# A mixture-of-experts layer behind a time-mixing layer: expert choice behind the scores, slot assignment behind the value mixes, GpSimd's scatters spread

## The chip, the cores and the metric

The kernel runs on one core of one Trainium2 chip. The metric is the device time in microseconds (us) of one execution, as the median of several. The engines of the core are named as in the profile: PE (TensorE, matmuls; PEld is its weight load), DVE (VectorE), ACT (ScalarE), POOL (GpSimd) and SP (SyncE, which issues most DMAs). Each has its own instruction stream and waits for others by semaphores.

## The reference, cut to what matters

```python
x = L0_attn_x                                # 8 x 512 x 512, float32
xn = _layernorm(x)
x = x + attn(xn) + ffn(xn)

# attn: prev = xn shifted by one step, xx = prev - xn
r, k, v, g = (xn + xx*tm_i) @ W_i.T          # four mixes, four 512 x 512 projections
# a scan over time of exp(k) and exp(k)*v, times sigmoid(r) and sigmoid(g), then @ Wo.T, layer norm

# ffn: z = w_norm * rmsnorm(xn), 4096 tokens
probs = softmax(z @ w_router)                # 32 experts
w_topk, sel = top_k(probs, 4)
pos = rank of a (token, choice) among those of its expert, in token order   # kept if pos < 256
y = (silu(buf @ w_gate) * (buf @ w_up)) @ w_down      # for each expert, on its up to 256 rows
out = sum of y over a token's experts by weight + sigmoid(z @ w_shared_gate) * shared_ffn(z)
```

## The kernel before, in words

The program has three stages, one after the other, each with a barrier of all engines at its end. The change lies in the first, `project_stage`; the second, `expert_stage`, begins by reading back from device memory the table of which token sits in which slot of which expert, gathers the rows of the first two experts by it, and transposes them. The third makes the shared part and the output.

The first stage runs over the 8 batches b of 512 tokens (round b); the first and last are written out, the rest are a loop of two rounds a turn. `one_round` of each engine's block is an instruction order written out by hand, so the order in the code is the order on the engine, and an instruction that waits holds all behind it on its engine.

All matmuls that need float32 precision are made as three matmuls of a high and a low part. For each of the four mixes i = K_, V_, R_, G_ and each of four chunks k: DVE makes `mixf` (`make_mix`), ACT rounds it to the high part (`mix_hi`), POOL subtracts to get the low part (`mix_lo`), and PE multiplies (`project`, in two halves, "pairs", of 24 matmuls each; pair 0 needs the low part of each chunk k in turn). What waits for what around the change:

- PE's order in round b: K pair 0, K pair 1, V pair 0, the two matmuls of `count(b)`, transposes `tz` and `ta` of token tile 0 of batch b+1, V pair 1, transposes of tile 1, R pair 0, `score(b+1, 0)`, transposes of tile 2, R pair 1, `score(b+1, 1)`, transposes of tile 3, G pair 0, `score(b+1, 2)` and `(b+1, 3)`, G pair 1. So the scores of a batch are complete one G pair before its own round.
- The four accumulators pj[m] are shared by all projections. K pair 0 of round b may write pj[0] and pj[1] only when DVE has read them in `make_gate(b-1, 0)` and `(b-1, 1)`.
- `choose(b)` on DVE (L540 to L564) turns scores into the four experts of each token and the running counts. `count(b)` on PE turns those into ranks. `assign(b)` on DVE (L576 to L598) makes slot numbers and weights. `scatter` on POOL then writes token numbers into their slots by 16 indirect DMAs a round.
- `norm_stats(b+1)` on DVE (L486, L489) feeds `norm_scales(b+1)` on POOL (L296 to L305), which stands ahead of the low parts of V of round b, since ACT needs the scales for `make_xn(b+1, ...)` and DVE then for `make_z(b+1, ...)` (L497), whose tile PE transposes.
- `route_exp(b)` on ACT takes the exponentials for the weights and needs what `choose(b)` leaves in `sh`.

The wait of PE for the accumulators is this:

```python
            def taken(b, i, m):
                if i == K_:
                    wait(pe, gate_made, b * 4 - 3 + m if not isinstance(b, int) or b else 0)
                else:
                    pe.wait_ge((None, ek_made, ekv_made, sr_made)[i], b * 4 + m + 1)
```

Of the kernel before, what the change touches and what calls it, by code (L numbers as in the profile page):

```python
# [28 lines left out]
KC = C // P  # L29
# [12 lines left out]
K_, V_, R_, G_ = range(4)  # L42
# [46 lines left out]
def project_stage(nc, keep, d):  # L89

    with ExitStack() as ctx:
# [192 lines left out]
        @block.gpsimd  # L284
        def _(pool):
            pows = Steps(pool, pow_step, POWS)

            def norm_scales(b):

                wait(pool, scales_kept, b)  # L290
                wait(pool, z_made, b * NT)
                wait_apart(pool, (setup_pool, 4), stats_step, (b + 1) * STATS)
                mean, var = mv[:, :, 0], mv[:, :, 1]
                rstd, shift = scales[:, 0:NT], scales[:, NT:2 * NT]
                pows.round(b)
                pows.link(pool.tensor_scalar(var_eps[:], var, EPS, None, ALU.add))  # L296
                pows.link(pool.tensor_tensor(rstd, var_eps[:], mhalf[:], ALU.pow))
                pows.step(pool.tensor_tensor(shift, mean, rstd, ALU.mult))
                pows.step(pool.tensor_tensor(var_eps[:], rstd, rstd, ALU.mult))
                pows.join_apart((setup_pool, 4))  # L300
                pows.step(pool.tensor_scalar(shift, shift, -1.0, None, ALU.mult))
                pows.step(pool.tensor_tensor(var_eps[:], var_eps[:], var, ALU.mult))
                pows.join_apart((setup_pool, 4))
                pows.link(pool.tensor_scalar(var_eps[:], var_eps[:], EPS_RMS, None, ALU.add))
                pows.step(pool.tensor_tensor(r2[:], var_eps[:], mhalf[:], ALU.pow))  # L305
                pows.end()

            def mix_lo(b, i, k):
                n = b * 16 + i * 4 + k
                pool.wait_ge(hi_made, n + 1)  # L310
                pool.tensor_tensor(mix[:, i % 2, k, 1, :], mixf[:, k, :], mix[:, i % 2, k, 0, :].bitcast(F32),  # L311
                                   ALU.subtract).then_inc(lo_made, 1)

            def scatter(b, first, last):

                if first == 0:
                    wait_apart(pool, (setup_pool, 4), slot_made, b + 1)
                for at in range(first, last):
                    pool.indirect_dma_start(  # L319
                        d["slots"], bass.IndirectOffsetOnAxis(ap=slot[:, at:at + 1], axis=0),  # L320
                        token[:, at // TOPK:at // TOPK + 1], None, bounds_check=SLOTS - 1, oob_is_err=False,
                    ).then_inc(scattered, 16)

            pool.memset(zero_tab[:], 0).then_inc(setup_pool, 1)
            pool.memset(mhalf[:], -0.5).then_inc(setup_pool, 1)
            pool.memset(ones[:], 1.0).then_inc(setup_pool, 1)
            pool.memset(seen[:], 0.0).then_inc(setup_pool, 1)
            pool.wait_ge(setup_pool, 4)
            norm_scales(0)
            for k in range(KC):  # L330
                mix_lo(0, K_, k)
            pool.wait_ge(table_zeroed, 16)

            def one_round(b, half, more, before):
                if more:
                    norm_scales(b + 1)
                for k in range(KC):
                    mix_lo(b, V_, k)
                for k in range(KC):
                    mix_lo(b, R_, k)  # L340
                scatter(b, 0, 4)
                for k in range(KC):
                    mix_lo(b, G_, k)
                scatter(b, 4, 12)
                if more:
                    for k in range(KC):
                        mix_lo(b + 1, K_, k)
                scatter(b, 12, 16)

            rounds(pool, one_round)  # L350
            pool.wait_ge(scattered, 16 * B * NT * TOPK)

        @block.scalar
        def _(act):
# [74 lines left out]
            def one_round(b, half, more, before):  # L429
                if before:  # L430
                    gate_g(b - 1, 2)
                    gate_g(b - 1, 3)
                for k in range(KC):
                    mix_hi(b, V_, k)
                exp_k(b, 0)
                exp_k(b, 1)
                if not before:
                    weight_hi(R_)
                if more:
                    make_xn(b + 1, 0)  # L440
                    make_xn(b + 1, 1)
                exp_k(b, 2)
                exp_k(b, 3)
                route_exp(b)
                for k in range(KC):
                    mix_hi(b, R_, k)
                if not before:
                    weight_hi(G_)
                if more:
                    keep_turned(b + 1, 1 - half, 0)  # L450
                    make_xn(b + 1, 2)
                    keep_turned(b + 1, 1 - half, 1)
                    make_xn(b + 1, 3)
                for k in range(KC):
                    mix_hi(b, G_, k)
                gate_r(b, 0)
                gate_r(b, 1)
                if more:
                    keep_turned(b + 1, 1 - half, 2)
                gate_r(b, 2)  # L460
                gate_r(b, 3)
                if more:
                    keep_turned(b + 1, 1 - half, 3)
                    mix_hi(b + 1, K_, 0)
                    mix_hi(b + 1, K_, 1)
                gate_g(b, 0)
                gate_g(b, 1)
                if more:
                    mix_hi(b + 1, K_, 2)
                    mix_hi(b + 1, K_, 3)  # L470
# [6 lines left out]
        def _(dve):  # L477
# [146 lines left out]
            for k in range(KC):  # L624
                make_mix(0, 0, K_, k)
            weight_lo(V_)

            def one_round(b, half, more, before):
                if more:
# [3 lines left out]
                    make_gate(b - 1, 3)  # L633
                for k in range(KC):
                    make_mix(b, half, V_, k)
                choose(b)
                if not before:
                    weight_lo(R_)
                make_mix(b, half, R_, 0)
# [9 lines left out]
                    z_lo(b + 1, 0)  # L649
                if not before:  # L650
                    weight_lo(G_)
                assign(b)
                make_ekv(b, 2)
                make_ekv(b, 3)
                if more:
# [9 lines left out]
                if more:  # L665
                    z_lo(b + 1, 2)
                    z_lo(b + 1, 3)
                    for k in range(KC):
                        shift_difference(b + 1, 1 - half, k)
                    make_mix(b + 1, 1 - half, K_, 0)  # L670
                    make_mix(b + 1, 1 - half, K_, 1)
                make_gate(b, 0)
                make_gate(b, 1)
                if more:
# [8 lines left out]
        def _(pe):  # L683
# [66 lines left out]

            def one_round(b, half, more, before):
                project(b, K_, 0)
                project(b, K_, 1)
                project(b, V_, 0)
                count(b)
                if more:
                    turn_z(b + 1, 0)
                    turn_xn(b + 1, 0)
# [992 lines left out]
```

## Time and profile before

| | us |
|---|---|
| median of 3 runs (1802.17 to 1803.08) | 1802.35 |
| the profiled execution, its own time | 1808.25 |
| its span, first to last instruction | 1806.4 |
| PE busy in the span | 1697.6 (94%) |
| DVE busy | 1239.6 (69%) |
| POOL busy | 872.0 (48%) |
| ACT busy | 662.2 (37%) |
| first stage, about | 0 to 488 |

Busy time is the sum over the whole span, and PE is nearly always busy. So what counts in the first stage is where PE stands still, and for whom. The granted clock, a mean over the span, is 0.973 of full speed.

### The profile page before, as it was taken

The numbers are of one execution on the slowest core, as the hardware profiler recorded it, in microseconds if no ns is written. First come the engines' busy times: TensorE is split into PE (matmuls) and PEld (weight loads), VectorE is DVE, ScalarE is ACT, GpSimd is POOL, SyncE is SP. The second block draws the span as 40 slices with busy tenths as digits, with TensorE's granted clock in tenths as the row PEclk, the third lists the DMA queues.
The fourth block names the chain that finished last, engine by engine and source line by source line (L and its number), as shares of the span: only waits on it lengthen the run. The fifth ranks groups of instructions, "written<-read, shape, count | busy, mean of one in ns | idle before, by whom it ended". The sixth has DMA issues, their size and how long they took to land. (4 is left out here: it accounts for less than half of the span.)

```text
span 1806.4 us, 26943 instructions
## 1 busy us (share of the span) xinstructions
PE 1697.6 (94%) x8752; PEld 1445.4 (80%) x8752; DVE 1239.6 (69%) x1798; ACT 662.2 (37%) x1083; POOL 872.0 (48%) x727
## 2 busy tenths in 40 slices
PE   4899999999589999999986889999999999999998
PEld 4687787778489999999974768888788888888887
DVE  4887787877255555555545778877686868777776
ACT  3444444454256656666642321212121211212121
POOL 2678777777644454454423524334252524334251
PEclk7999999999889999999997999999999999999999
DMA  6233333333276666666637665455554443343431
GB/s 221 94 136 129 134 139 141 139 116 116 103 257 225 231 251 229 226 250 235 221 112 265 192 204 179 150 198 174 165 164 139 151 147 110 110 161 117 141 108 50
DMA packets 130475, 299.43 MB, mean 166 GB/s; under 512 B 23692, under 2 KB 35212, under 8 KB 129872
## 3 DMA queue, kind: packets, MB, share of 16 engines
q1 hardware_dynamic: 110928, 264.64, 41.6%
q0 software_dynamic: 19456, 33.67, 6.6%
q8 instruction: 45, 0.74, 0.2%
q14 instruction: 46, 0.38, 0.1%
HBM read 233.64 MB, written 81.36 MB: 174 GB/s over the span
## 5 line engine op out<-in xcount | busy, mean ns | idle before, releaser
L738 PE MATMUL pj<-mix,w 128*128 128x512 f32 x1536 | 377.7, 403 | 14.1 <-POOL mix L311 12.2
L738 PEld LDWEIGHTS pj<-mix,w 128*128 128x128 f32 x1536 | 290.0, 191 | 87.1 <-issue 10.7
L1616 PE MATMUL s_gp<-s_zT,s_wg 128*128 128x512 f32 x1056 | 265.1, 402 | 38.4 <-DVE s_wg L1524 22.3
L1616 PEld LDWEIGHTS s_gp<-s_zT,s_wg 128*128 128x128 f32 x1056 | 204.6, 195 | 85.1 <-DVE s_wg L1524 25.1
L1630 PE MATMUL s_yp<-s_wd,s_h 128*128 128x512 f32 x1056 | 254.1, 390 | 0.6 <-DVE s_h L1433 0.6
L1616 PE MATMUL s_up<-s_zT,s_wu 128*128 128x512 f32 x1056 | 253.9, 389 | 0.0
L1630 PEld LDWEIGHTS s_yp<-s_wd,s_h 128*128 128x128 f32 x1056 | 198.1, 188 | 42.6 <-issue 1.2
L1616 PEld LDWEIGHTS s_up<-s_zT,s_wu 128*128 128x128 f32 x1056 | 198.7, 188 | 41.5
L876 POOL TENSOR_TENSOR e_wg<-e_g_in,e_wg 128x1408 fp32r<-128x1408 f32 x32 | 103.5, 3233 | 214.4 <-ACT e_wg L896 214.4
L311 POOL TENSOR_TENSOR mix<-mixf,mix 128x512 fp32r<-128x512 f32 x128 | 174.1, 1389 | 67.4 <-ACT mix L385 67.2
L1275 POOL DMA_INDIRECT s_picked<-y_rows,s_slot x128 | 144.3, 1128 | 83.8 <-DVE s_total L1483 45.6
L319 POOL DMA_INDIRECT slot_tokens<-token,slot x128 | 134.0, 1047 | 63.6 <-issue 36.5
L1348 ACT ACTIVATE s_act_g<-s_gp 128x512 f32<-128x512 f32 x88 | 52.5, 597 | 301.5 <-PE s_gp L1616 294.9
L1034 PE MATMUL e_gu<-e_xT,e_wg 128*128 128x256 f32 (+1 forms) x1152 | 153.4, 283 | 2.4 <-DVE e_xT L980 2.4
L1034 PE MATMUL e_gu<-e_xT,e_wu 128*128 128x256 f32 (+1 forms) x1152 | 152.5, 282 | 0.0
L1359 ACT ACTIVATE s_h<-s_act_g 128x512 fp32r<-128x512 f32 x88 | 55.5, 631 | 259.5 <-DVE s_act_g L1427 250.9
L1034 PEld LDWEIGHTS e_gu<-e_xT,e_wg 128*128 128x128 f32 (+1 forms) x1152 | 145.4, 181 | 5.4 <-DVE e_xT L980 2.8
L385 ACT ACTIVATE mix<-mixf 128x512 fp32r<-128x512 f32 x128 | 80.8, 633 | 185.0 <-DVE mixf L521 151.9
L1034 PEld LDWEIGHTS e_gu<-e_xT,e_wu 128*128 128x128 f32 (+1 forms) x1152 | 142.6, 180 | 0.0
L1057 PE MATMUL e_yp<-e_wd,e_h 128*128 128x512 f32 (+1 forms) x576 | 140.1, 396 | 0.0
L1483 DVE SCALAR_TENSOR_TENSOR s_total<-s_picked,s_rec,s_total 128x512 f32<-128x512 f32 x128 | 135.4, 1058 | 3.4
L1057 PEld LDWEIGHTS e_yp<-e_wd,e_h 128*128 128x128 f32 (+1 forms) x576 | 106.3, 189 | 21.4
(148 smaller groups left out, 2392.1 us busy)
## 6 DMA issues: line engine op xcount, KB each, us to landing
s_wu<-wu_split SPq DMA_DIRECT2D x77, 512.0 KB
e_g_in<-in_w_gate SPq DMA_DIRECT2D x32, 704.0 KB
e_u_in<-in_w_up SPq DMA_DIRECT2D x32, 704.0 KB
zT_tiles<-zT SPq DMA_DIRECT2D x32, 512.0 KB
e_d_in<-in_w_down SPq DMA_DIRECT2D x32, 512.0 KB
y_rows<-e_y SPq DMA_DIRECT2D x32, 512.0 KB, 2.9
s_zT<-zT_tiles SPq DMA_DIRECT2D x32, 512.0 KB, 5.8
x_in<-in_x SPq DMA_DIRECT2D x32, 256.0 KB
```

The costliest lines, as they stand in the source:

```text
L311: pool.tensor_tensor(mix[:, i % 2, k, 1, :], mixf[:, k, :], mix[:, i % 2, k, 0, :].bitcast(F32), ALU.subtract).then_inc(lo_made, 1)
L319: pool.indirect_dma_start(d["slots"], bass.IndirectOffsetOnAxis(ap=slot[:, at:at + 1], axis=0), token[:, at // TOPK:at // TOPK + 1], None, ...
L385: act.activation(mix[:, i % 2, k, 0, :], mixf[:, k, :], ACT.Copy).then_inc(hi_made, 1)
L738: last = pe.matmul(pj[m][:], w[i][:, w_part, k, m * P:(m + 1) * P], mix[:, i % 2, k, x_part, :], start=(k == 0 and q == 0), stop=(k == KC ...
L876: pool.tensor_tensor(wg[:, half, 1, :], g_in[:, half, :], wg[:, half, 0, :].bitcast(F32), ALU.subtract).then_inc(wg_lo, 1)
L1034: last = pe.matmul(gu[f][0:m, which, :], w[:, half, w_part, k * F + f0:k * F + f0 + m], xT[:, half, x_part, k, :], start=(q == 0 and k == ...
L1057: last = pe.matmul(yp[c][:], h[0:m, f, h_part, c * P:(c + 1) * P], wd[0:m, half, w_part, f, :], start=(f == 0 and q == 0), stop=(f == NF - ...
L1275: pool.indirect_dma_start(picked[:, k, :], None, d["y_flat"], bass.IndirectOffsetOnAxis(ap=slot[:, j * TOPK + k:j * TOPK + k + 1], axis=0) ...
L1359: act.activation(h[:, i, 0, :], act_g[:, i, :], ACT.Copy).then_inc(h_hi, 1)
L1483: dve.scalar_tensor_tensor(total[:, j, :], picked[:, k, :], rec[:, at:at + 1], total[:, j, :], ALU.mult, ALU.add).then_inc(picked_used, 1)
L1616: last = pe.matmul(bank[:], parts[w_part][:, k, :], zT[:, :, x_part, k, :], start=(q == 0 and k == 0), stop=(q == 2 and k == KC - 1))
L1630: last = pe.matmul(yp[j][:], h[:, i, h_part, j * P:(j + 1) * P], wd[:, w_part, f, :], start=(f == 0 and q == 0), stop=(f == NFS - 1 and q ...
```

## The change

It reorders instructions and adds or removes none. On DVE `choose(b+1)` moves from behind the V mixes of its own round into the round before, right behind the first two K mixes of b+1 and ahead of `make_gate(b, 0)` and the other two K mixes; for the first batch it stands ahead of the first round. `assign(b)` takes the place that `choose(b)` had. `count(b)` on PE moves from behind V pair 0 to between the two K pairs. On ACT `route_exp(b)` moves ahead of the exponentials of the second K pair. On POOL the scatters, which stood in blocks of 4, 8 and 4 (behind the R low parts, the G low parts and the K low parts of b+1), now stand as 3, 2, 4, 2 and 5, between pairs of low parts, all ahead of the K low parts of b+1.

```diff
 # POOL, one_round
                 for k in range(KC):
                     mix_lo(b, V_, k)
-                for k in range(KC):
-                    mix_lo(b, R_, k)
-                scatter(b, 0, 4)
-                for k in range(KC):
-                    mix_lo(b, G_, k)
-                scatter(b, 4, 12)
+                scatter(b, 0, 3)
+                mix_lo(b, R_, 0)
+                mix_lo(b, R_, 1)
+                scatter(b, 3, 5)
+                mix_lo(b, R_, 2)
+                mix_lo(b, R_, 3)
+                scatter(b, 5, 9)
+                mix_lo(b, G_, 0)
+                mix_lo(b, G_, 1)
+                scatter(b, 9, 11)
+                mix_lo(b, G_, 2)
+                mix_lo(b, G_, 3)
+                scatter(b, 11, 16)
                 if more:
                     for k in range(KC):
                         mix_lo(b + 1, K_, k)
-                scatter(b, 12, 16)
 # ACT, one_round
                 exp_k(b, 1)
+                route_exp(b)
...
                 exp_k(b, 3)
-                route_exp(b)
 # DVE, ahead of the rounds and in one_round
             weight_lo(V_)
+            choose(0)
...
                 for k in range(KC):
                     make_mix(b, half, V_, k)
-                choose(b)
+                assign(b)
...
                 if not before:
                     weight_lo(G_)
-                assign(b)
                 make_ekv(b, 2)
...
                     make_mix(b + 1, 1 - half, K_, 0)
                     make_mix(b + 1, 1 - half, K_, 1)
+                    choose(b + 1)
                 make_gate(b, 0)
                 make_gate(b, 1)
 # PE, one_round
                 project(b, K_, 0)
+                count(b)
                 project(b, K_, 1)
                 project(b, V_, 0)
-                count(b)
```

DVE's order at the end of the first round (`xx` is the shifted difference, `mixf` a mix, `sr` the gate product, `lg` to `seen` the choice). Before:

```order
L507 TENSOR_TENSOR zT<-tz,zT 128x512 x2
L513 TENSOR_TENSOR xx<-xnT 128x512 x4
L521 SCALAR_TENSOR_TENSOR mixf<-xx,tm,xnT 128x512 x2
L533 TENSOR_TENSOR sr<-sr,pj 128x512 x2
L521 SCALAR_TENSOR_TENSOR mixf<-xx,tm,xnT 128x512 x2
```

And now, with lines of the changed file:

```order
L527 SCALAR_TENSOR_TENSOR mixf<-xx,tm,xnT 128x512 x2
L546 COPY lg<-rp 128x136
L548 TENSOR_TENSOR lg<-lg,rp 128x136
L551 MAX v<-lg 128x8 x4
L554 MAX_INDEX i<-v,lg 128x8 x4
...
L562 TENSOR_TENSOR oh<-idxf,const 128x512
L566 TENSOR_REDUCE chosen<-oh 128x128
...
L570 TENSOR_TENSOR seen<-seen,chosen 128x32 x4
L539 TENSOR_TENSOR sr<-sr,pj 128x512 x2
L527 SCALAR_TENSOR_TENSOR mixf<-xx,tm,xnT 128x512 x2
```

The whole choice now stands ahead of the two gate products and of the last two K mixes.

DVE's order behind the V mixes of the first round. Before, the choice and then, after the low part of a weight (`w`), the R mixes and the tiles `z`:

```order
L521 SCALAR_TENSOR_TENSOR mixf<-xx,tm,xnT 128x512 x4
L540 COPY lg<-rp 128x136
...
L564 TENSOR_TENSOR seen<-seen,chosen 128x32 x4
L612 TENSOR_TENSOR w<-sr,w 128x2048
L521 SCALAR_TENSOR_TENSOR mixf<-xx,tm,xnT 128x512 x2
L497 SCALAR_TENSOR_TENSOR z<-xn,r,norm_w 128x512 x2
```

And now:

```order
L527 SCALAR_TENSOR_TENSOR mixf<-xx,tm,xnT 128x512 x4
L582 TENSOR_TENSOR oh<-oh,rp 128x512
L584 TENSOR_REDUCE pos<-oh 128x16
L585 TENSOR_SCALAR valid<-pos 128x16
...
L604 COPY keep_rec<-rec 128x20
L618 TENSOR_TENSOR w<-sr,w 128x2048
L527 SCALAR_TENSOR_TENSOR mixf<-xx,tm,xnT 128x512 x2
L503 SCALAR_TENSOR_TENSOR z<-xn,r,norm_w 128x512 x2
```

The assignment, two instructions on 512 elements and 15 on a few, stands where the choice stood; what follows is the same.

POOL's order in the first round, from its last scale (`r`) on (`mix` a low part, `slot_tokens` a scatter). Before:

```order
L305 TENSOR_TENSOR r<-var_eps,mhalf 128x4
L311 TENSOR_TENSOR mix<-mixf,mix 128x512 x8
L319 DMA slot_tokens<-token,slot 8192x1 x4
L311 TENSOR_TENSOR mix<-mixf,mix 128x512 x4
L319 DMA slot_tokens<-token,slot 8192x1 x8
L311 TENSOR_TENSOR mix<-mixf,mix 128x512 x4
L319 DMA slot_tokens<-token,slot 8192x1 x4
```

And now:

```order
L311 TENSOR_TENSOR mix<-mixf,mix 128x512 x4
L319 DMA slot_tokens<-token,slot 8192x1 x3
L311 TENSOR_TENSOR mix<-mixf,mix 128x512 x2
L319 DMA slot_tokens<-token,slot 8192x1 x2
L311 TENSOR_TENSOR mix<-mixf,mix 128x512 x2
L319 DMA slot_tokens<-token,slot 8192x1 x4
L311 TENSOR_TENSOR mix<-mixf,mix 128x512 x2
L319 DMA slot_tokens<-token,slot 8192x1 x2
L311 TENSOR_TENSOR mix<-mixf,mix 128x512 x2
L319 DMA slot_tokens<-token,slot 8192x1 x5
L311 TENSOR_TENSOR mix<-mixf,mix 128x512 x4
```

No scatter stands between the K low parts of the next batch and its scales any more; 3 stand ahead of the R low parts, and 5 of the 16, not 12, behind the last G low part.

## Rows read from the trace of the kernel before

**Rows 1.** Who PE waited for, 40 to 480 us: total, times, longest

```profile
PE pj L738 <- POOL mix L311: 8.5, 5, 2.0
```

**Rows 2.** PE's timeline: start, us, engine, line, what, count, idle before

```profile
121.60 0.23 PE L717 MATMUL rp<-chosen,before 128*128 128x128 bf16 x1
...
225.75 5.86 PE L738 MATMUL pj<-mix,w 128*128 128x512 f32 x24 [1.98 <-POOL mix L311]
...
260.19 1.87 PE L708 MATMUL rp<-wr,zT 128*128 128x68 f32 x16
261.90 17.04 PE L738 MATMUL pj<-mix,w 128*128 128x512 f32 x72
280.74 7.41 PE L738 MATMUL pj<-mix,w 128*128 128x512 f32 x24 [1.80 <-POOL mix L311]
...
397.57 0.23 PE L717 MATMUL rp<-chosen,before 128*128 128x128 bf16 x1
...
450.04 0.23 PE L717 MATMUL rp<-chosen,before 128*128 128x128 bf16 x1
```

**Rows 3.** A stretch behind a wait: us, PE busy (x), PEclk, DMA share, GB/s

```profile
282.00:285.40 3.40, 3.40 (x9) 0.50 0.00 0
```

**Rows 4.** POOL's timeline behind the K low parts, round 3

```profile
214.60 0.99 POOL L319 DMA_INDIRECT slot_tokens<-token,slot  x1 [0.15 <-issue]
...
219.65 0.50 POOL L296 TENSOR_SCALAR var_eps<-mv 128x4 f32<-128x4 f32 x1
...
224.36 5.02 POOL L311 TENSOR_TENSOR mix<-mixf,mix 128x512 fp32r<-128x512 f32 x4
```

**Rows 5.** DVE's timeline: the choice (round 1), and around it and assignment (round 3)

```profile
108.62 0.29 DVE L540 COPY lg<-rp 128x136 f32<-128x136 f32 x1
...
113.16 0.81 DVE L564 TENSOR_TENSOR seen<-seen,chosen 128x32 bf16<-128x32 bf16 x4
...
224.45 4.96 DVE L564 TENSOR_TENSOR seen<-seen,chosen 128x32 bf16<-128x32 bf16 x4
229.33 1.40 DVE L521 SCALAR_TENSOR_TENSOR mixf<-xx,tm,xnT 128x512 f32<-128x512 f32 x2
230.66 2.43 DVE L497 SCALAR_TENSOR_TENSOR z<-xn,r,norm_w 128x512 f32<-128x512 f32 x2
...
237.79 0.68 DVE L576 TENSOR_TENSOR oh<-oh,rp 128x512 f32<-128x512 f32 x1
...
241.49 0.18 DVE L598 COPY keep_rec<-rec 128x20 f32 x1
...
262.05 1.28 DVE L533 TENSOR_TENSOR sr<-sr,pj 128x512 f32<-128x512 f32 x2 [1.25 <-issue]
```

**Rows 6.** ACT's high parts, 40 to 480 us, by line: busy, mean ns, idle

```profile
L385 ACT ACTIVATE mix<-mixf 128x512 fp32r<-128x512 f32 x124 | 78.3, 633 | 180.0 <-DVE mixf L521 147.0 <-issue 30.6
```

**Rows 7.** One line of DVE: duration ns least/median/most, first and last start

```profile
L578 DVE TENSOR_REDUCE pos<-oh x8: 685/686/686, 73.1 to 454.0; 128x16 f32<-128x512 f32 x8
```

**Rows 8.** Timelines of DVE and PE in the first round

```profile
43.47 2.46 DVE L486 BATCH_NORM_STATS2 st<-x_in 128x6 f32<-128x512 f32 x4
...
52.84 5.96 PE L738 MATMUL pj<-mix,w 128*128 128x512 f32 x24 [1.44 <-issue]
...
57.72 2.28 DVE L612 TENSOR_TENSOR w<-sr,w 128x2048 fp32r<-128x2048 f32 x1
...
62.04 0.75 PE L690 MATMUL tz<-const,z 128*128 128x128 f32 x4 [3.12 <-DVE z L497]
...
89.33 0.72 PE L690 MATMUL ta<-const,xn 128*128 128x128 f32 x4 [2.61 <-ACT xnT L372]
89.81 5.52 PE L738 MATMUL pj<-mix,w 128*128 128x512 f32 x16
```

**Rows 9.** The end of the stage: POOL's last scatter, and who SP waited for

```profile
484.40 0.97 POOL L319 DMA_INDIRECT slot_tokens<-token,slot  x1 [0.30 <-issue]
...
SPq L91 <- PEq L91: 3.8, 1, 3.8
```

## The prediction

> **What bounds the kernel now.** PE is busy for 94% of the span, so I read only its gaps. The list of who PE waited for gives the recurring one: five waits for POOL's low parts, 8.5 us together [rows 1]. PE's timeline puts them at the start of V pair 0 (225.75, 280.74) [rows 2]. What all gaps of the steady rounds cost follows from the repeating `count`: from 121.60 to 397.57 there are five intervals, 55.2 us each; the one to 450.04 takes 52.47, with the same matmuls and no wait ahead of V [rows 2]. So the five lose 5 x 2.73 = 13.6 us. About 8.5 are the waits; another 1.6 is the V pair behind one of them, 7.41 us where 225.75 shows 5.86 [rows 2]: PE's granted clock there is 0.50, the lower of its levels (1.2 GHz), right after it had stood still for 1.80 [rows 2, 3].
>
> Why PE waits is in POOL's timeline: four scatters from 214.60, the scales from 219.65, the first V low part from 224.36, 1.3 us long, when PE had been ready since 223.8 [rows 4]. In the last round the scales fall away, and so does the wait.
>
> **The change, part by part.** I count from E, the end of the last score of the next batch (262.06) [rows 2]. DVE's gate products started there at 262.05 [rows 5]. PE starts K pair 0 5.5 us behind E (a third of the 17.04 from 261.90) [rows 2].
>
> *The choice behind the scores.* It takes 108.62 to 113.97, 5.35 us, when POOL is not in low parts [rows 5]. Two K mixes, two gates and PE stand behind it. Gates: E+5.35 to E+6.65 (1.28 for two). K mixes 2 and 3, 0.7 each [rows 5]: E+7.35 and E+8.05. High part 0.63 [rows 6], low part 1.27 (5.02 for four) [rows 4], plus about 0.1 a hop: low part 2 at E+9.5, low part 3 at E+10.8. PE: first wait for the gate, start E+6.05, chunk 2 at E+9.5 where it would have been at 5.5+2.8 = E+8.3, chunk 3 at E+10.9, done E+12.35 for 11.2 without waits. **K pair 0 ends 1.1 us late in each of rounds 1 to 7: +7.7.** The choice meets only K low parts 0 and 1 on POOL, until about E+1.4. Its first instructions then read PSUM or one operand, and such ones were never held: the reduce L578 takes 685 to 686 ns in all rounds [rows 7]. The bound above is one held for those low parts, +0.75; below, a whole hidden half, if gates alone count, 0.5 in place of 1.1.
>
> *The V wait.* No scatters stand between the K low parts and the scales. Statistics follow K mix 3 (2.9 us as from 43.47 in the first round [rows 8]): E+11.0. Scales 4.7 (219.65 to 224.36) [rows 4]: E+15.7; V low part 0: E+17.0. PE, late as above, wants it at E+18.1. Covered, by 1.1 us. **All that the five intervals lose goes: -13.6.** If the cover is gone, part of the waits returns.
>
> *The assignment behind the V mixes.* Undisturbed it is 3.9 us, 237.79 to 241.67 [rows 5]. It starts at E+14.9, and POOL is in V low parts from E+15.7 to E+20.9. Short DVE instructions are held then: the four `seen` additions, 0.81 us alone, took 4.96 beside the low parts of 224.36 [rows 4, 5]. I therefore let only the first two and about four short instructions pass by E+20.9; 2.1 us are left. Behind them stand R mixes 0 and 1 (1.4) and the first `z` (0.75): ready at E+25.2. PE wants it when V pair 0 ends, E+18.1+5.7 = E+23.8. **A new wait of 1.3 to 1.4 us ahead of the transposes, in six rounds: +7.8.** Before, there was no such wait but no slack either: V pair 0 from 225.75 ended at 231.5, and `z` was there at 231.4 [rows 2, 5]; the difference is that the choice ended with the low parts, and the assignment has a tail beyond them. Bounds: 0 (the short ones slip through) to 2.1.
>
> The Trainium skill's page SBUF — State Buffer, section Who interferes with whom, has this as an exclusive port pair held for one whole instruction, against DVE's two-input and 2-port forms, with reduces free of it. The `seen` and reduce rows agree. Taken strictly, assignment loses a little less there than I charge, some 2 us over six rounds.
>
> *Scatters and what else moves.* 16 scatters a round of about 1.28 us each (start to start: four fill 214.60 to 219.65 [rows 4]) are the same work. Five of them behind the last G low part leave POOL free before the K high parts come, where eight did not; three ahead of the R low parts delay these by 3.8 us, some 4 us before PE wants them. `route_exp` finds its input long made. `count` between K pairs finds the choice made in rounds 1 to 7. All at nothing.
>
> *First round.* `choose(0)` now stands ahead of the statistics, which began at 43.47 [rows 8]. They end at 43.47+5.35+2.9 = 51.7, the scales at 56.4, V low part 0 at 57.7 for a V pair that started at 52.84 [rows 8]. PE stands still twice on the way (for the choice, ahead of `count(0)`, and for this). Then the low parts to 61.5, the rest of the assignment 1.0 (much of it passes before 56.4), the weight's low part 2.3 [rows 8], mixes 1.4, `z` 0.7: 66.9, where the transposes started at 62.04 [rows 8]: +4.9. The assignment is gone from the rest of the round, so the wait of 2.61 at 89.33 should go, and with it the slow 16 matmuls behind it, 5.52 where full clock gives 3.9 [rows 8]. **+4.9 - 2.6 - 1.6 = +0.7.** Bounds -2 to +5.
>
> *End of the stage.* POOL's last scatter begins at 484.40, and SP, done with its own, waits 3.8 us for the barrier [rows 9]. With 7 scatters fewer at the end (9 us) POOL is done before SP: **-3.8.**
>
> **Sum.** 7.7 + 7.8 - 13.6 + 0.7 - 3.8 = -1.2. The profiled execution took 1808.25 (span 1806.4), 5.9 above the median; all terms are differences in it, so I set them against the median: 1802.35 - 1.2 = **1801.2 us**. About 0.2%, 3.6 us, is what a measurement of this kernel tells from no change.
>
> **The rivals.**
>
> *The waits balance* (forecast, 0.42): 1797 to 1806. V waits of some 2.7 a round become 1.1 + 1.3.
>
> *The assignment slips through* (0.26): its short instructions run between low parts and no `z` wait arises. For it: DVE did get turns between low parts. Against: `seen`. Gives -1.2 - 7.8 = -9.0, 1793.3.
>
> *The clock falls more often* (0.18). PE now stands still twice a round, 13 times. Before, one of five waits of 1.4 to 2.0 us brought the lower clock, at 1.55 us [rows 2, 3]. Mine are shorter, and I charge none. If half of them bring it: 6 x 1.55 = +9.3, 1810.5.
> The page TensorE: Matmul & The Clock Gate of the same skill, section HAM oscillation — how this bites in real kernels, describes recurring waits that lower the clock each time; by that all 13 would, +20, which the trace so far doesn't bear out (one in five).
>
> *The choice is held on DVE* (0.14), the slower side in one mechanism: it stands ahead of what PE needs next, and K low parts 0 and 1 run as it begins. Held for 0.75 us it costs 7 x 0.75 = +5.2 (1806.5); held for both, 2.5 us, 7 x 2.5 = +17.5 (1818.7). It decides from 0.7 us a round on. For it: `seen`. Against: the kinds of instruction that come first.
>
> **Chances and range.** Faster by over 0.2% (below 1798.7): the slipping case and a tenth of the forecast's spread, 0.31. Within: 0.40. Slower (above 1806.0): the clock and the held choice, less their mild ends, 0.29. The range for 8 in 10 runs from the slipping case to the clock case, 1793 to 1810; the forecast's own is 1797 to 1806.
>
> **What would show it.** In the changed profile: no wait of PE for POOL ahead of V pair 0; ahead of K pair 0 one for DVE's gate and one for a K low part, together 1.1; one of 1.3 for `z` ahead of the transposes; `count` intervals of 54.9 us; SP's wait at the end gone. It is wrong if the interval comes out at 53.6 (no `z` wait) or above 56 (choice held, or the lower clock granted behind the new waits), or if the first round loses over 5 us.

## The result, and the profile after

The changed kernel takes **1808.49 us** (median of 18 runs, 1804.65 to 1811.28), the kernel before, run beside it, 1804.42 us (18 runs, 1802.17 to 1809.05). The ratio is 1.0022, 95% interval 1.0015 to 1.0029: slower by 0.22%, about 4 us, where no change to speak of was forecast (1801.2 us; 1808.5 lies within the range of 1793 to 1810).

The page's head and its row for PE:

```profile
span 1806.4 us, 26943 instructions
PE 1701.1 (94%) x8752; PEld 1445.0 (80%) x8752; DVE 1212.2 (67%) x1798; ACT 662.4 (37%) x1083; POOL 880.5 (49%) x727
```

The span is the same, to the tenth, as that of the profiled execution of before. Here that says nothing: the profiled execution of before (1808.25 us) lay far above its kernel's median, this one (1808.26 us) on its own. The stage that was changed has to be compared step by step, and with more than one execution of before.

Who PE waited for from 40 to 480 us, in total, times, longest, to be read against [rows 1] and [rows 8]; then who SP waited for at the end of the stage, against [rows 9]:

```profile
PE tz L697 <- DVE z L503: 4.9, 6, 2.0
PE pj L745 <- POOL mix L311: 4.8, 10, 1.5
PE pj L745 <- DVE sr L539: 4.7, 7, 2.4
PE rp L724 <- DVE seen L570: 4.2, 1, 4.2
...
SPq L91 <- PEq L91: 0.2, 1, 0.2
```

Of the 8.5 us of waits for POOL ahead of V pair 0, in five places, two waits of 0.3 are left; the rest of the 4.8 is six short waits within K pair 0 and two in the last round. Three new kinds stand there: DVE's gates seven times, `z` six times (2.04 in the first round, which waited for it before too, and five times later), the first choice once. SP hardly waits at the end. PE's timeline shows what a round looks like now (start, us, what, idle before and its releaser):

```profile
49.19 0.29 PE L724 MATMUL rp<-chosen,before 128*128 128x128 bf16 x1 [4.22 <-DVE seen L570]
...
66.14 0.75 PE L697 MATMUL tz<-const,z 128*128 128x128 f32 x4 [2.04 <-DVE z L503]
...
104.54 7.41 PE L745 MATMUL pj<-mix,w 128*128 128x512 f32 x24 [2.40 <-DVE sr L539]
111.78 0.23 PE L724 MATMUL rp<-chosen,before 128*128 128x128 bf16 x1
...
268.96 3.06 PE L745 MATMUL pj<-mix,w 128*128 128x512 f32 x12 [0.34 <-DVE sr L539]
272.26 3.06 PE L745 MATMUL pj<-mix,w 128*128 128x512 f32 x12 [0.24 <-POOL mix L311]
...
287.12 0.75 PE L697 MATMUL tz<-const,z 128*128 128x128 f32 x4 [0.42 <-DVE z L503]
...
384.68 0.23 PE L724 MATMUL rp<-chosen,before 128*128 128x128 bf16 x1
...
438.98 0.23 PE L724 MATMUL rp<-chosen,before 128*128 128x128 bf16 x1
...
460.39 11.46 PE L745 MATMUL pj<-mix,w 128*128 128x512 f32 x48 [1.49 <-POOL mix L311]
473.19 8.67 PE L745 MATMUL pj<-mix,w 128*128 128x512 f32 x36 [1.33 <-POOL mix L311]
```

A steady round (268.96, 272.26, 287.12) has the waits that were forecast: for the gate ahead of K pair 0, for a low part in its middle, for `z` ahead of the transposes. A wait costs more than its idle time. From the start of G pair 1 (262.77) to that of K pair 1 (275.26) it is 12.49 us; in the kernel before the same two pairs take 11.28, and `count` between them adds 0.10. That leaves 1.1 us for two waits with 0.58 us of idle time, so some 0.25 us come on top of each, which the rows show as busy. I call it draining; what it consists of the trace does not tell. Three places were not in the forecast: the gate's wait of 2.40 in round 1, with 24 matmuls of 7.41 us behind it (the others: 5.85), the lower clock behind the wait for the first choice, and two waits for POOL in the last round. The second of them, as a stretch (us, PE busy, PEclk; K pair 1 runs in it, and takes 8.14 us):

```profile
47.60:54.40 6.80, 5.21 (x14) 0.50 0.00 0
```

For the comparison I take, per kernel, the starts of `count` of each batch, and their distances:

| execution | from the second `count` on | first interval |
|---|---|---|
| before, [rows 2] | 54.66 55.20 56.53 54.16 55.42 52.47 | 62.96 |
| before, second (`before_again`) | 54.59 53.96 54.01 53.98 54.59 52.46 | 62.80 |
| before, third (`before_third`) | 54.60 53.96 54.53 53.93 54.61 52.46 | 62.94 |
| after | 53.57 54.32 55.49 54.30 55.22 54.30 | 62.59 |
| after, second (`after_again`) | 54.28 54.33 55.35 54.32 55.16 54.30 | 61.53 |

The distances of 56.53 and 55.42 that the prediction was made from are not there in the other two executions of before.

### The profile page after: what moved, and what is told of

It is laid out like the page before. It is cut to its first block and busy times, and to the rows that moved or that the text cites. A ratio compares the mean times of both kernels' runs of the same rounds, so it can differ in the third digit from the quotient of the medians.

```text
span 1806.4 us, 26943 instructions
## 1 busy us (share of the span) xinstructions
PE 1701.1 (94%) x8752; PEld 1445.0 (80%) x8752; DVE 1212.2 (67%) x1798; ACT 662.4 (37%) x1083; POOL 880.5 (49%) x727
## 5 line engine op out<-in xcount | busy, mean ns | idle before, releaser
L311 POOL TENSOR_TENSOR mix<-mixf,mix 128x512 fp32r<-128x512 f32 x128 | 164.5, 1317 | 70.0 <-ACT mix L391 69.6
L319 POOL DMA_INDIRECT slot_tokens<-token,slot x128 | 144.4, 1128 | 39.2 <-issue 37.8
```

The source lines that it names most:

```text
L319: pool.indirect_dma_start(d["slots"], bass.IndirectOffsetOnAxis(ap=slot[:, at:at + 1], axis=0), token[:, at // TOPK:at // TOPK + 1], None, ...
```

## The experiments

The question was where a gain of 13.6 us in the steady rounds had gone. The theories: the loss sits in the steady rounds (new waits at K and `z`), in round 1 (the choice held on DVE), or in the last round (scatters between the low parts). In kernels with `EARLY` and `SPREAD` the three flags are for the first, the middle and the last round, and switch the order of choice and assignment, and that of the scatters.

**The kernel before once more.** No edit.

> The kernel before, unchanged. The two profiled executions have the same span (1806.4 us) while the medians lie 4 us apart, so one of the profiles is not typical. Theory 1: the one of before is long by some 4 us, because of spells of the lower clock (three in its first stage); then this profile shows a span near 1802 to 1804, and the ratio of times is 1.000. Rival: the spans of profiles say nothing of the median and this one is 1806 again.

Measured: 1803.67 us, ratio 0.9998 (0.9988 to 1.0007). What PE waited for in its profile, 40 to 480 us:

```profile
PE pj L738 <- POOL mix L311: 5.4, 5, 1.4
PE tz L690 <- DVE z L497: 3.8, 2, 3.1
PE ta L690 <- ACT xnT L372: 2.6, 1, 2.6
```

Its profiled execution took 1802.74 us, with a span of 1800.9, so the first profile was the long one. The V waits come to 5.4 us, not 8.5, and PE's granted clock falls behind none of them, where it fell once in the first profile; the excess is thus mostly not the clock. The five steady intervals add up to 271.13 us, 8.8 more than 5 x 52.46. In the first profile DVE also stands for 1.46 and 1.65 us ahead of the statistics of rounds 3 and 5, with no releaser; in this one it does not. A third execution was taken for its intervals:

> The kernel before, a third profile. The forecast took from the first profile that five steady rounds lose 13.6 us; the second showed 8.8 (intervals of 54.0 to 54.6 us). Theory 1: the first was the odd one, this one shows 8 to 10 us again. Rival: the rounds really scatter between executions, and it lies anywhere from 8 to 14.

Its time was 1804.18 us, and its five lose 9.3. So there were about 9 us to be had from the steady rounds, not 13.6. Likewise the changed kernel again:

> The changed kernel, a second profile. Theory 1: the steady intervals repeat within 0.2 us (54.3, 55.5, 54.3, 55.3, 54.3), the last round has its two waits for R and G low parts (2.8 us) again, and the wait of 2.4 us for the gate in round 1, which hangs on how late POOL is there, lies between 1.2 and 2.5. Rival: any of these was of that one execution.

Its time was 1810.84 us. The waits stand in the same places, the gate's in round 1 too (2.39 us), this time with no slow matmuls behind it. The slow K pair 1 behind the first choice is there again (0.50 of the clock from 49 to 54).

**The choice behind the K mixes.** It tells what the choice costs where the change put it.

```diff
                     make_mix(b + 1, 1 - half, K_, 1)
-                    choose(b + 1)
                 make_gate(b, 0)
                 make_gate(b, 1)
                 if more:
                     make_mix(b + 1, 1 - half, K_, 2)
                     make_mix(b + 1, 1 - half, K_, 3)
+                    choose(b + 1)
```

> The changed kernel with the choice behind both gates and all four K mixes, still in the round before. Theory 1: the K waits (0.6 us a round, and 2.4 in round 1 with the lower clock behind it) go; but statistics and scales come some 4 us later against PE, so V low part 0 is late by some 2 us a round in rounds 1 to 6: in all 5 to 10 us slower than the changed kernel. Rival (the K waits are what counts): 6 us faster than it.

Measured: 1818.03 us, 1.0076 (1.0063 to 1.0090). The choice now delays the gates of the second half, which PE wants ahead of K pair 1:

```profile
PE pj L745 <- DVE sr L539: 12.8, 5, 3.9
```

The place that the change chose is the cheaper of the two. The kernel is 9.5 us above the changed one, within the 5 to 10 expected, but not for the reason expected: the V waits did not grow, PE waits 2.8 us for POOL in all. Two of the gate waits, 3.86 and 3.88 us, are 3 us longer than the two of 0.83 and 0.82 in the rounds behind them; in those two rounds DVE stands for 2.97 and 2.92 us with no releaser ahead of the statistics.

**The scatters as before.** The other half of the change undone.

```diff
-                scatter(b, 0, 3)
-                mix_lo(b, R_, 0)
...
-                scatter(b, 11, 16)
+                for k in range(KC):
+                    mix_lo(b, R_, k)
+                scatter(b, 0, 4)
+                for k in range(KC):
+                    mix_lo(b, G_, k)
+                scatter(b, 4, 12)
                 if more:
                     for k in range(KC):
                         mix_lo(b + 1, K_, k)
+                scatter(b, 12, 16)
```

> The changed kernel with the scatters of before (4, 8 and 4, the last four behind the K low parts). Theory 1: the last four scatters, 5.1 us, push the scales and V low part 0 from 17.0 to 22 us behind the end of the scores, where PE wants it at 18: a wait of 3 to 4 us ahead of V in rounds 1 to 6 and the clock falling behind some of them, so 15 to 25 us slower than the changed kernel. Rival (the scatters' places don't matter in the steady rounds): within 3 us of it.

Measured: 1832.87 us, 1.0154 (1.0138 to 1.0170). PE waits for POOL at V again, longer than before, and the lower clock comes back; the second fence is a stretch behind such a wait (us, PE busy, PEld, DVE, ACT, POOL, PEclk):

```profile
294.99 5.30 PE L739 MATMUL pj<-mix,w 128*128 128x512 f32 x15 [3.09 <-POOL mix L311]
```

```profile
295.00:299.00 4.00, 4.00 (x11) 3.15 (x12) 4.00 (x3) 2.61 (x5) 4.00 (x3) 0.57 0.00 0
```

The early choices with the old places of the scatters cost 28 us over before, within what was expected: four scatters still stand between the K low parts and the scales, and the statistics behind the choice come later than they did. The spread is what makes the move bearable.

**The scatters of the last round as before.**

```diff
+                if not more:
+                    for k in range(KC):
+                        mix_lo(b, R_, k)
+                    scatter(b, 0, 4)
+                    for k in range(KC):
+                        mix_lo(b, G_, k)
+                    scatter(b, 4, 16)
+                    return
                 scatter(b, 0, 3)
```

> The changed kernel, but in the last round all R low parts stand ahead of the first scatter and all G low parts behind the fourth, as before. Theory 1 (the last round's scatters between low parts cost PE 2.8 us of waits for R and G low parts, 3.2 us in all): faster than the changed kernel by 3 us, so level with before or up to 1 us above it; both waits gone; the gain at the stage's end stays. Rival (the 13 small waits of the steady rounds make the change slower): no more than 1 us faster than the changed kernel, 3 to 4 us slower than before.

Measured: 1805.93 us, 1.0011 (1.0002 to 1.0020). The changed kernel, measured in other runs, stands at 1.0022 (1.0015 to 1.0029) to the same kernel before; by these ratios it gains 2 us, and the two intervals overlap. PE runs through from 454.81 to its end, where the changed kernel stood still twice, 2.8 us together; SP waits 1.8 us again (3.3 to 3.8 before, 0.2 in the changed kernel), so not all of the gain at the end of the stage stays. In the traces the last round's R and G pairs are 3.3 us shorter and the end is 1.7 longer:

```profile
454.81 23.26 PE L753 MATMUL pj<-mix,w 128*128 128x512 f32 x99
```

```profile
SPq L91 <- PEq L91: 1.8, 1, 1.8
```

What POOL does there in the changed kernel:

```profile
445.99 0.99 POOL L319 DMA_INDIRECT slot_tokens<-token,slot  x1 [1.45 <-DVE slot L592]
451.77 0.98 POOL L319 DMA_INDIRECT slot_tokens<-token,slot  x1 [4.79 <-issue]
...
459.06 2.52 POOL L311 TENSOR_TENSOR mix<-mixf,mix 128x512 fp32r<-128x512 f32 x2
...
471.85 2.53 POOL L311 TENSOR_TENSOR mix<-mixf,mix 128x512 fp32r<-128x512 f32 x2
```

Behind the first scatter POOL stands for 4.79 us with no releaser, and the R low parts queue behind it: the last two end at 461.6, while PE had been ready for the first of them at 458.9. The G low parts are late in the same way. In the kernel before the R low parts stand ahead of the scatters, and the stop, 2.93 us there, holds up nothing that PE waits for.

**One stage of the change at a time.** The first round alone, the steady rounds alone, the last alone (its three last rounds written out instead of looped, with the scatters of before), and first and last together:

```diff
-                choose(b)
+                if early(b, more, before):
+                    assign(b)
+                else:
+                    choose(b)
...
+        EARLY = (True, False, False); SPREAD = (True, False, False)    # first_round_only
+        EARLY = (False, True, True);  SPREAD = (False, True, False)    # steady_only
+        EARLY = (False, False, True); SPREAD = (False, False, False)   # last_round_only
+        EARLY = (True, False, True);  SPREAD = (True, False, False)    # first_and_last
```

> The kernel before, with the change in the first round alone: choice of batch 0 ahead of the round, its assignment behind the V mixes, count(0) between the K pairs, the scatters of round 0 spread; all later rounds as before. Theory 1 (the first round, forecast at +0.7 us, is a gain: the changed kernel's profile has the first G pair 1 start 2.5 us earlier than the kernel before): 2.5 us faster than before, ratio 0.9986. Rival (what is gained before round 1 is given back there, since POOL's scatters run late into the K low parts of batch 1): ratio 1.000.

> The changed kernel with the first round of before (choice, count and scatters of batch 0 at their old places) and the last round's scatters in the old order; the choices of batches 1 to 7 are still made a round ahead. Theory 1 (steady rounds lose 0.7 to 1.2 us at K and up to 0.8 at z and win back the V wait, which in a typical execution is 0.5 to 1.5 and not the 2.7 a round of the first profile): count intervals of 54.3 to 55.5 us against 54.0 to 54.6, so the stage is 4 to 5 us longer, the end gives back 3: 1 to 2 us slower than before. The forecast's term (13.6 us lost before, 15.5 after) would make it 2 us faster, end of the stage included.

> The kernel before, with only the last batch's choice made a round ahead and its assignment behind the V mixes; scatters in the old order; rounds 5 to 7 are written out instead of 7 alone. Theory 1: K pair 0 of the last round 0.6 to 1.1 us late, SP's wait at the end of the stage (3.3 to 3.8 us) gone or nearly: 2 to 2.5 us faster than before. Rival (the last scatters are bound by POOL's own work, not by when slots are known): no gain, or slower through code that is no loop.

> Both of the last two edits together, the steady rounds as before. If the parts add up as theory 1 has it: 4.5 to 5 us faster than before, ratio 0.9973, and faster than the changed kernel by 9. Rival (they overlap or the written-out rounds cost): within 2 us of before.

| kernel | median us | ratio to before | 95% |
|---|---|---|---|
| `first_round_only` | 1801.20 | 0.9983 | 0.9974 to 0.9992 |
| `steady_only` | 1812.38 | 1.0047 | 1.0034 to 1.0060 |
| `last_round_only` | 1807.60 | 1.0018 | 1.0009 to 1.0026 |
| `first_and_last` | 1805.36 | 1.0008 | 0.9999 to 1.0017 |

Only the first of these expectations held. `steady_only` is 8 us slower where 1 to 2 were expected, `last_round_only` 3 us slower where a gain of 2 was, and `first_and_last` 1 us slower where a gain of 4.5 to 5 was.

The first round gains 3 us by itself in the medians. In its one profile PE is 3.0 us ahead of `before_again` at the last G pair of the first round, 2.0 at that of round 1 and 1.6 at the end of the stage, so part is given back in rounds 1 and 2, as the rival had it. Its PE waits 3.7 us for the first choice, but the wait of 2.61 for `xnT` [rows 8] has become 0.3 and that of 3.12 for `z` [rows 8] is 0.4 (2.0 in `first_and_last`, whose first round is the same):

```profile
PE rp L755 <- DVE seen L594: 3.7, 1, 3.7
...
PE tz L728 <- DVE z L527: 0.9, 2, 0.4
PE ta L728 <- ACT xnT L399: 0.3, 1, 0.3
```

The steady rounds alone lose. Their first one, 5.8 us longer than in `before_again`, meets POOL still behind with the 4, 8, 4 of round 0 and waits at V as never before:

```profile
120.36 2.07 PE L776 MATMUL pj<-mix,w 128*128 128x512 f32 x4 [3.19 <-POOL mix L320]
```

and from round 2 on they are 0.5 to 0.6 us a round longer than in `before_again`. The last round alone loses 3 us: its scatters begin at 452.48, and POOL stands even longer behind the first, so that the last one begins at 481.91 (478.87 in `before_again`) and SP's wait is 4.3. Rounds 5 and 6 are written out in it as well; what that does by itself no run shows:

```profile
452.48 0.99 POOL L330 DMA_INDIRECT slot_tokens<-token,slot  x1 [0.15 <-issue]
459.09 0.98 POOL L330 DMA_INDIRECT slot_tokens<-token,slot  x1 [5.62 <-issue]
```

**Scatters moved, choice left.** If the V wait is POOL's lateness, two scatters behind the last K low part in place of four should take it without any early choice.

```diff
+                if more:
+                    for k in range(KC):
+                        mix_lo(b, R_, k)
+                    scatter(b, 0, 4)
+                    mix_lo(b, G_, 0)
+                    mix_lo(b, G_, 1)
+                    scatter(b, 4, 5)
+                    mix_lo(b, G_, 2)
+                    mix_lo(b, G_, 3)
+                    scatter(b, 5, 13)
+                    mix_lo(b + 1, K_, 0)
+                    mix_lo(b + 1, K_, 1)
+                    scatter(b, 13, 14)
+                    mix_lo(b + 1, K_, 2)
+                    mix_lo(b + 1, K_, 3)
+                    scatter(b, 14, 16)
+                    return
```

> The kernel before, choices and assignments where they were; only the scatters of rounds 0 to 6 placed anew: 4 behind the R low parts, 1 between the pairs of G low parts, 8 behind them, 1 between the pairs of K low parts, and 2 in place of 4 ahead of the scales. Theory 1 (the V wait is POOL's four scatters and the scales): V low part 0 comes 2.6 us earlier, the V wait of 0.7 to 1.6 us in rounds 1 to 6 goes: 5 to 8 us faster than before, ratio 0.996. Rival (the wait comes from the statistics, or is handed on to z, which had no slack): 2 us or less.

> The last one and the change of the first round together. If they add: 8 to 11 us faster than before, ratio 0.995. Rival: the spread scatters of round 0 already took their part, and the sum is 2 us short.

Measured: 1800.73 us, 0.9973 (0.9963 to 0.9983), and with the first round's change added 1800.90 us, 0.9983 (0.9972 to 0.9993). Both are ahead of both kernels of this case; the two don't add, and both gains fall short of what was expected (5 to 8, and 8 to 11 us). The V waits only shrink:

```profile
PE pj L755 <- POOL mix L311: 4.6, 6, 0.8
PE ta L707 <- ACT xnT L389: 2.8, 7, 1.4
```

Compared pair by pair with `before_again`, the profile of `scatters_two_behind_k` is 2.5 us ahead at the last G pair of the first round, gives back 1.4 in round 1, and rounds 2 to 7 save 1.3: they give back at `xnT` most of what they save at V. The 2.5 is not shown to be the edit's work, since two kernels with the first round of before reach that G pair at 97.13 (`before_third`) and 96.80 (`last_round_only`), not at 98.79. POOL's scatters are thus not all of the V wait, and where the 4.4 us of the median come from is shown only in part.

## Why the prediction was wrong, step by step

Against the kernel before, the starts of PE's matmul pairs in the changed kernel give this budget. The stage ends with SP's first load of the second stage. There are two executions of each kernel with typical steady rounds, so the budget can be made twice:

| place | forecast | `after` to `before_again` | `after_again` to `before_third` |
|---|---|---|---|
| first round, to its last G pair | +0.7 | -2.5 | -1.1 |
| round 1 | K 1.1, `z` 1.3: +2.4 | +4.0 | +2.0 |
| rounds 2 to 7, up to the last R pair | K 6 x 1.1, `z` 5 x 1.3, V -13.6: -0.5 | +3.6 | +3.0 |
| last round, R and G pairs | 0 | +3.3 | +3.3 |
| end of the stage | -3.8 | -3.2 | -3.2 |
| sum | -1.2 | +5.3 | +4.0 |

The medians differ by 4.1 us (1808.49 to 1804.42). How the loss up to the end of round 1 (+1.5 and +0.9) splits over the two rounds hangs on the execution of before: its last G pair of round 0 begins at 98.79 or at 97.13, that of round 1 at 151.46 or at 151.50.

- **The steady loss, -13.6, is the term that failed first.** It was read from one execution whose rounds 3 to 5 were long. The other two show 8.8 and 9.3. In `before_again` it is made of five waits, 5.4 us with 0.25 of draining each, and 0.4 within each V pair behind them (24 matmuls in 6.23 to 6.33 us, not 5.85). With 9 in its place the same sum gives +3.4, a loss. The prediction saw that its profiled execution was 5.9 us above the median and set differences of it against the median; part of the excess was in the term itself.
- **The new wait at K, +7.7:** right in place, releasers and size from round 2 on. 0.34 and 0.24 us idle, with the draining 1.1 us a round.
- **The wait for `z`, +7.8:** in place, but in five rounds and not six (six in `after_again`), and the idle time is 0.43 and 0.81 us by turns, 0.7 and 1.2 with the draining, where 1.3 was charged. DVE's timeline beside POOL's low parts, from 279.06 to 284.15, shows why it is less:

```profile
279.23 1.15 DVE L588 SCALAR_TENSOR_TENSOR s<-idxf,bad 128x16 f32<-128x16 f32 x1
...
280.60 1.06 DVE L591 CAST token<-const 128x4 uint32<-128x4 f32 x1
...
281.66 1.27 DVE L594 TENSOR_SCALAR tot<-ex 128x4 f32<-128x4 f32 x1
...
283.39 0.79 DVE L598 TENSOR_TENSOR rec<-ex,rtot 128x16 f32<-128x16 f32 x1
```

  Four instructions are held, each for about one low part; between them one or two pass. The prediction let six through by the end of the low parts, and 13 of the 17 had gone. This is half of the rival "the assignment slips through".
- **The V wait:** the cover was there in every second round; in the others 0.3 us is left. The changed kernel's five intervals that answer to the five of before add up to 272.90 us, 10.6 more than 5 x 52.46: K 5 x 1.1, `z` about 4, V 2 x 0.5. So 8.8 went and 10.6 came. What is left at V no longer waits for scatters: POOL, done with the K low parts, waits 0.4 us for DVE's statistics, and in the longer rounds 1.3 to 1.6. In those, rounds 3 and 5, DVE stands still ahead of the statistics where its loop of two rounds turns:

```profile
216.46 2.47 DVE L492 BATCH_NORM_STATS2 st<-x_in 128x6 f32<-128x512 f32 x4 [1.12 <-issue]
```

  It is 1.12 and 0.86 us in the changed kernel, 1.00 and 0.81 in `after_again`, and the intervals that contain these rounds are longer than those around them by 1.2 and 0.9, and 1.0 and 0.8. So 2 of the 10.6 us are this stop, which was in no term of the sum; every kernel here with early choices in the steady rounds has it, `before_again` and `before_third` do not. What stops DVE the trace doesn't name. Forecast were 54.9 us an interval; they are 54.6. The nearness is luck in part, since `z` was charged too much and the stop not at all. The mistake lies in what they were compared with.
- **The choice held on DVE** was given 0.14 for all rounds. It happened in one, for the rest of both low parts, about the 2.5 us that the rival charges a round. The instruction held, L556, has a single input. That "such ones were never held" was read from one reduce, and rows of the kernel before already spoke against it: a TENSOR_SCALAR that mostly takes 174 ns took 1148 once.

```profile
L579 DVE TENSOR_SCALAR valid<-pos x8: 174/174/1148, 73.8 to 454.7; 128x16 f32<-128x16 f32 x8
```

  In round 1 of the changed kernel, POOL's K low parts and the choice beside them:

```profile
98.13 2.57 POOL L311 TENSOR_TENSOR mix<-mixf,mix 128x512 fp32r<-128x512 f32 x2
```

```profile
98.47 2.27 DVE L556 TENSOR_SCALAR sh<-lg 128x4 f32<-128x4 f32 x1
...
103.80 1.28 DVE L539 TENSOR_TENSOR sr<-sr,pj 128x512 f32<-128x512 f32 x2
```

  In round 3 the same low parts are through 1.7 us after the last score, and L556, 2.0 us after it, takes 0.15. In round 1 POOL comes 2.5 us later against the score. Three of round 0's scatters took 3.09, 1.41 and 3.04 us in place of 0.97, and all 16 together 4.0 us more than those of round 3. "About E+1.4" was true of the steady rounds and had no spare; the prediction did not follow POOL through round 0. `first_round_only` has the same slow scatter (3.10 us), no choice of batch 1 where it could be held, and gains. That the slow scatters are what makes POOL late in round 1 is argued from these numbers; no run removed them alone. That POOL's time is what counts there, `last_round_old_scatters` shows, whose rounds 0 and 1 are those of the changed kernel. In its execution the choice began 0.9 us later, while POOL's low parts began 0.3 earlier; it was held for 1.00 and not 2.27, PE waited 1.20 and not 2.40, and K pair 0 began at 104.26 all the same (104.54 and 104.24 in the two of the changed kernel). So between executions of one order of instructions, what PE gains in round 0 it loses again in round 1, and the two lines of the budget belong together.

```profile
99.40 1.00 DVE L564 TENSOR_SCALAR sh<-lg 128x4 f32<-128x4 f32 x1
```

```profile
104.26 3.05 PE L753 MATMUL pj<-mix,w 128*128 128x512 f32 x12 [1.20 <-DVE sr L547]
```

- **The last round** was costed at nothing, with "three scatters ahead of the R low parts delay these by 3.8 us, some 4 us before PE wants them". That holds where the R pairs stand behind transposes of the next batch, and where scatters follow one another at 1.28 us. The last round has no next batch, so PE comes sooner, and its first scatter is followed by a stop of 4.79 us. `last_round_old_scatters` takes the two waits away and gains 2 us by the ratios, since 1.7 of the 3.3 come back at the end of the stage.
- **The end of the stage, -3.8,** was right, to 0.6 us (SP's wait 3.3 to 3.8 before, 0.2 now). But it and the 3.3 us above it are one trade: PE ends later against POOL because it waited for POOL's low parts between the scatters. With the old scatters in the last round alone half of it stays (SP waits 1.8); with an early choice in the last round alone none does (4.3), behind a stop of POOL of 5.62 us, so the shares of choice and spread are not separated.
- **The first round, +0.7,** was too high: -2.5 and -1.1, about the lower bound of -2. The wait for the first choice and the end of the `xnT` wait with its slow matmuls came as said. What was not foreseen goes both ways. PE waits 4.2 us for the choice, and the clock falls behind that: K pair 1 takes 8.14 us, 2.3 more than at full clock, in `after_again` too. On the other side `z` is late by 2.04 where it was by 3.12, and with that a low spell is gone: the granted clock was 0.50 from 63.0 to 66.4 in `before_again` and is 1.00 now. A wait of 0.70 for `z` at 78.54 is gone too. `before_third` shows how loose this term is: its clock was 0.50 from 77.7 to 84.5 instead, and it waited 2.18 us for `z` where `before_again` waited 0.70 for `z` and 2.60 for `xnT`.
- **The clock** fell behind two of the 25 waits from 40 to 480 us in the changed kernel (to 0.50, the lower level of 1.2 GHz): behind that of 4.22 for the first choice and that of 2.40 in round 1. In `after_again` it fell behind the first choice alone (3.99), not behind 2.39. It fell behind none of the waits of 0.2 to 0.8 us that the change brought in the steady rounds, so the rival's half of them was far off. In `old_scatters` it fell at V in five rounds, behind waits of 2.8 to 3.1 us, but not behind one of 3.19 in round 1; in `choose_after_k` three times, behind 3.39, 3.86 and 3.88. The Trainium skill's page TensorE: Matmul & The Clock Gate, section HAM oscillation — how this bites in real kernels, has recurring waits lower the clock each time, in a kernel whose waits for DMAs took about 3 to 5 us. `choose_after_k` and `old_scatters` agree with that, but for the one of 3.19. The prediction carried it over to 13 waits of at most 1.3 us, for which the page does not say it.

## What to carry to other kernels

A gain that is a difference between rounds should be read from two or three executions, before it is put against costs of the same size; here 4 to 5 us of 13.6 belonged to one execution. A reordering that is right in the loop is to be followed separately through the first round, through the one behind it and through the last, since queues stand elsewhere there: here 2.0 to 4.0 us were lost in round 1 and 3.3 in the last, against 3.0 to 3.6 in the rounds between. And where one engine's place in a queue is the problem, moving that engine's work alone (here the scatters, 0.27% faster) is worth trying before work of a second engine is moved with it.

## What the runs showed that I had not expected

- POOL stands still between the first and the second scatter of the last round in every kernel, with no releaser in the trace: 2.93 us in all three executions of before, in `last_round_old_scatters` and four other kernels, 4.79 in the changed kernel, 4.36 in `choose_after_k`, 5.60 to 5.62 in `old_scatters`, `first_and_last` and `last_round_only`. Elsewhere the gap is 0.30. In the longer ones SP had issued a load of 1 MB (`wkv_in`) 0.6 to 1.8 us before the stop began; where it is 2.93 no load was issued that shortly before. Whether that is the cause, and what POOL waits for, is open; no run here was made for it.
- A scatter of POOL takes 3.09 us, not 0.97, while DVE computes the low part of a whole weight (128x2048, from 60.72). It was so in the changed kernel, its second execution (3.10) and `first_round_only` (3.10), and in each a second time:

```profile
72.31 3.04 POOL L319 DMA_INDIRECT slot_tokens<-token,slot  x1 [0.30 <-issue]
```

```profile
72.22 2.28 DVE L618 TENSOR_TENSOR w<-w_in,w 128x2048 fp32r<-128x2048 f32 x1
```

  Here DVE takes the 2.28 us that it takes undisturbed [rows 8]: only POOL loses. The 3.38 us of the first one fit a wait for the V low part that POOL was in until 61.96, not for the scatter.
- A wait of PE costs some 0.25 us more than the idle time that the trace shows (1.1 us for two waits with 0.58 us idle).
- Executions of one kernel differ by up to 2.5 us in a single round, with the same instructions in the same order (56.53 and 54.01 for the same interval of before).
